# A spatial gate's edge sums on one Trainium2 core: two passes of four-tile groups, or one pass of twelve-tile batches in order of source

## The reference, cut to what matters

```python
h = x @ gcn_w                                   # one score per node
deg = segment_sum(ones, dst) ; dis = rsqrt(deg) # with one more self loop
msg = h[src] * (dis[src] * dis[dst])[:, None]
spa = sigmoid(segment_sum(msg, dst) + gcn_b)
return x * spa + x + x * gate                   # gate: a small MLP on the mean row of x
```

## Time and profile before

| | us |
|---|---|
| median of 3 runs | 8108.09 (8104.7 to 8108.87) |
| the profiled execution's own time | 8111.77 |
| its span (first to last instruction) | 8110.0 |
| mean granted PE clock over the span | 0.731 |

### The profile page before, as it was taken

One profiled execution on the slowest core, in us unless ns is written; L12 is line 12 of the kernel. 1 busy time (PEld: TensorE's weight loads), 2 busy tenths in 40 slices (PEclk: granted clock), 3 DMA queues, 4 the chain that ended last, 5 costly groups with the idle time before them and its releaser, 6 DMA issues. The chain is left out here.

```text
span 8110.0 us, 144759 instructions
## 1 busy us (share of the span) xinstructions
PE 5676.6 (70%) x26332; PEld 3710.7 (46%) x26333; DVE 5077.9 (63%) x16894; ACT 1922.6 (24%) x2930; POOL 4449.1 (55%) x5024
## 2 busy tenths in 40 slices
PE   5566667799999866629999997944555555555550
PEld 4333334477777646516555554522333333333330
DVE  8877777477777579866777775556333333333335
ACT  4100000288888323202333332310000000000000
POOL 0477777377777300002777771001777777777770
PEclk7577777899999865559999999977555555555555
DMA  2244444433333200013333333001111113111122
GB/s 86 59 123 122 123 125 130 117 108 103 103 103 102 50 4 0 0 36 98 104 104 104 104 103 65 0 23 52 52 52 52 52 52 50 52 52 52 52 50 64
DMA packets 306083, 583.62 MB, mean 72 GB/s; under 512 B 88467, under 2 KB 175708, under 8 KB 305562
## 3 DMA queue, kind: packets, MB, share of 16 engines
q0 software_dynamic: 185408, 469.86, 21.3%
q1 hardware_dynamic: 120538, 112.45, 4.5%
HBM read 544.78 MB, written 43.61 MB: 73 GB/s over the span
## 5 line engine op out<-in xcount | busy, mean ns | idle before, releaser
L1591 DVE TENSOR_TENSOR acc<-bank,acc 128x256 f32 (+1 forms) x3552 | 1273.4, 358 | 1725.6 <-PE bank L732 1356.4
L732 PE MATMUL bank<-ring,oh 128*128 128x128 f32 x3552 | 1335.8, 485 | 937.9 <-issue 647.1
L732 PEld LDWEIGHTS bank<-ring,oh 128*128 128x128 f32 x3552 | 885.0, 312 | 1388.8 <-issue 1006.4
L497 POOL CAST stage_i<-s_idx 128x8 int32 (+1 forms) x224 | 46.3, 206 | 1773.3 <-DMA q_table<-hq 1044.9
L512 POOL DMA_INDIRECT ring<-h_table,stage_i x888 | 858.4, 967 | 255.7 <-PE bank L805 149.0
L512 POOL DMA_INDIRECT ring<-fwd_table,stage_i x888 | 847.2, 954 | 261.4 <-issue 230.2
L512 POOL DMA_INDIRECT ring<-bwd_table,stage_i x888 | 847.9, 955 | 258.5 <-issue 232.5
L512 POOL DMA_INDIRECT ring<-q_table,stage_i x888 | 845.2, 952 | 262.5 <-issue 140.7
L1143 ACT ACTIVATE ring<-big 128x889 f16<-128x889 f16 x840 | 874.0, 1041 | 214.1 <-PE bank L816 182.1
L816 PE MATMUL bank<-ring,big 128*128 128x445 f16 (+1 forms) x3360 | 773.7, 352 | 0.0
L1602 DVE TENSOR_SCALAR oh<-iota,d_loc,d_norm 128x128 f32<-128x128 f32 x1776 | 651.8, 370 | 70.1 <-DVE big L1675 20.3
(11 more groups left out here) (394 smaller groups left out, 8402.7 us busy)
## 6 DMA issues: line engine op xcount, KB each, us to landing
big<-places_in_block SPq DMA_DIRECT2D x111, 256.0 KB
ring<-h_table,stage_i POOLq DMA_INDIRECT x888
ring<-q_table,stage_i POOLq DMA_INDIRECT x888
ring<-fwd_table,stage_i POOLq DMA_INDIRECT x888
ring<-bwd_table,stage_i POOLq DMA_INDIRECT x888
big<-x_and_degree,stage_i POOLq DMA_INDIRECT x536
h_table<-hq SPq DMA_DIRECT2D x50, 128.0 KB, 1.7
x_table<-big SPq DMA_DIRECT2D x1, 6400.0 KB, 20.3
```

Source lines behind the costliest of these rows:

```text
L732: pe.matmul(bank[u % 4][:, 0:width], oh[:, u % 4, :], gbuf[:, u % RING, 0:width], start=True, stop=True).then_inc(S["mm"], 1)
L1591: dve.tensor_tensor(to, bank[u % 4][:, 0:width], to, ALU.add).then_inc(S["accd"], 1)
```

## The change

The two passes, `node_values` and `segment_sums` with `combine`, become one pass, `node_sums`, over the list in order of source, in 74 batches of 12 tiles. For each batch: SP loads the 1536 source places to all 128 partitions as a row (`load_slots`, 384 KB, two buffers); DVE compares it with the partition's number (`slot_oh`, one operation of 1536 columns); PE fetches the values with 12 matmuls of three columns at the tile's block (`slot_values`); ACT copies them in pairs (`copy_values`); DVE compares the destination's block (600 columns, `high_eq`) and place (1536 columns, `low_oh`) with `iota`, and multiplies the block one-hot by the three parts of the values in one operation of 12 x 3 x 50 = 1800 columns (`place_values`); PE adds 12 products of 150 columns to `bank[7]` (`slot_sums`). At the end three operations add the three parts.

`read_codes` moves from DVE to POOL in 32-bit float operations, behind POOL's last gather of the second pass: 15 linked operations until `s_ready` is 1, and 7 more until it is 2 (destination's place and block, in pairs). Before the mean's sums PE now clears `bank[7]` and transposes `s_loc` (7 transposes), and ACT copies the result (`slot_w`), ahead of its first square root; SP stores it to `places_in_block`. The scores of a pair are made after the normalisation of the next one (`node_scores(i - 1)` behind `normal_rows(i)`), with waits on semaphores of an earlier turn. `gate_bc` and `gate_done` move behind `spa_in`, and with them SP's load of the next layer's weights.

The core of the diff (the lines between are left out):

```diff
-        code_i = [spare(2 * SLOTS + TC * k, TC)[:, 0:T].bitcast(I32) for k in range(3)]
+        code_f = [spare(2 * SLOTS + TC * k, T) for k in range(3)]
...
+        EDGES = BATCH * P
+        slot_rows, slot_oh = (acc_flat[:, a:a + EDGES].bitcast(BF16).rearrange("p (k n) -> p k n", k=2) for a in (0, EDGES))
...
@@ SP @@
+            sp.wait_ge(S["slot_w_ready"], 2)
+            sp.dma_start(loc_dram.rearrange("(g p n) -> p g n", p=P, n=P), slot_w.rearrange("p (g n) -> p g n", n=P)).then_inc(S["locs_out"], 16)
...
+            def load_slots(i, k, first):
+                if not first:
+                    sp.wait_ge(S["slot_sel"], i * 2 + k - 1)
+                sp.dma_start(slot_rows[:, k, :], loc_dram[ds(i * (2 * EDGES) + k * EDGES, EDGES)].partition_broadcast(P)).then_inc(rows_in[k], 16)
...
             sp.wait_ge(S["gate_done"], 1)
@@ POOL @@
+            pool.wait_ge(S["sort_out"], 4)
+            for k in range(2):
+                link(pool.tensor_tensor(diffs[k], raised[k][:, 1:T + 1], raised[k][:, 0:T], ALU.subtract))
...
+            def by_128(low, high, whole):
+                link(pool.tensor_scalar(high, whole, 1.0 / P, -63.5 / P, ALU.mult, ALU.add))
+                link(pool.tensor_scalar(high, high, ROUND, None, ALU.add))
+                link(pool.tensor_scalar(high, high, ROUND, None, ALU.subtract))
+                link(pool.tensor_scalar(low, high, -float(P), None, ALU.mult))
+                link(pool.tensor_tensor(low, whole, low, ALU.add))
...
+            pool.sem_inc(S["s_ready"], 1)
+            by_128(code_lo, code_hi, s_idx[:, 0:T])
+            for to, code in ((dst_lo, code_lo), (dst_hi, code_hi)):
+                link(pool.tensor_copy(to, code.unsqueeze(2).to_broadcast([P, T, 2])))
+            pool.sem_inc(S["s_ready"], 1)
@@ PE @@
-            def segment_sums(k):
-            def combine(k, turns):
-            def node_values(k):
...
+            def slot_values(i, k):
+                b = i * 2 + k
+                pe.load(slot_regs, blk_s[0:1, ds(i * (2 * BATCH) + k * BATCH, BATCH)])
+                pe.wait_ge(S["slot_sel"], b + 1)
+                pe.wait_ge(S["slot_cp"], b + 1)
+                for u in range(BATCH):
+                    block_no = pe.snap(slot_regs[u], min_val=0, max_val=NB - 1)
+                    mm = pe.matmul(bank[2 + k][:, u * 4:u * 4 + 3], slot_oh[:, k, u * P:(u + 1) * P],
+                                   table3[:, :, ds(block_no, 1)].rearrange("p s a -> p (s a)"), start=True, stop=True)
+                mm.then_inc(S["slot_val"], 1)
+
+            def slot_sums(i, k):
+                pe.wait_ge(S["slot_prod"], i * 2 + k + 1 + 2)
+                for u in range(BATCH):
+                    mm = pe.matmul(bank[7][:, 0:3 * NP], low_oh[k][:, u, :], high_val[k][:, u, :], start=False, stop=False, skip_group_check=True)
+                mm.then_inc(S["slot_acc"], 1)
+
+            def node_sums():
...
+                with pe.Fori(1, BATCHES // 2) as i:
+                    slot_values(i, 0)
+                    slot_sums(i - 1, 1)
+                    slot_values(i, 1)
+                    slot_sums(i, 0)
...
+            pe.wait_ge(S["s_ready"], 1)
+            for g in range(TG):
+                mm = pe.transpose(bank[g // 4][:, g % 4 * P:(g % 4 + 1) * P], s_loc[:, g * P:(g + 1) * P], ident[:, :])
+            mm.then_inc(S["pe_chain"], 1)
+            pe.wait_ge(S["slot_w_ready"], 2)
@@ ACT @@
+            def copy_values(i, k):
+                b = i * 2 + k
+                act.wait_ge(S["slot_val"], b + 1 + 2)
+                act.wait_ge(S["slot_prod"], b + 1)
...
+            act.wait_ge(S["pe_chain"], 1)
+            for h in range(2):
+                n = (4 if h == 0 else TG - 4) * P
+                act.activation(slot_w[:, h * 4 * P:h * 4 * P + n], bank[h][:, 0:n], ACT.Copy).then_inc(S["slot_w_ready"], 1)
             square_root(sm["rstd"][:, 0:NBE])
@@ DVE @@
+            def select_slots(i, k):
+                b = i * 2 + k
+                dve.wait_ge(rows_in[k], i * 16 + LOADED[k] + 16)
+                dve.wait_ge(S["slot_val"], b + 1)
+                dve.tensor_scalar(slot_oh[:, k, :], slot_rows[:, k, :], node_no[:, :], None, ALU.is_equal).then_inc(S["slot_sel"], 1)
+                t = ds(i * (2 * BATCH) + k * BATCH, BATCH)
+                dve.wait_ge(S["slot_acc"], b + 1)
+                dve.tensor_tensor(by_pairs(high_eq[k], NP), iota_pairs(NP), over(dst_hi[:, t, :], NP), ALU.is_equal).then_inc(S["slot_eq"], 1)
+                dve.tensor_tensor(by_pairs(low_oh[k], P), iota_pairs(P), over(dst_lo[:, t, :], P), ALU.is_equal)
+
+            def place_values(i, k):
+                b = i * 2 + k
+                dve.wait_ge(S["slot_cp"], b + 1 + 2)
+                dve.wait_ge(S["slot_eq"], b + 1)
+                o = dve.tensor_tensor(high_val[k].rearrange("p u (s n r) -> p u s n r", s=3, r=2),
+                                      by_pairs(high_eq[k], NP).unsqueeze(2).to_broadcast([P, BATCH, 3, NP // 2, 2]),
+                                      val_pairs[k].unsqueeze(3).to_broadcast([P, BATCH, 3, NP // 2, 2]), ALU.mult)
+                o.then_inc(S["slot_prod"], 1)
...
+                with dve.Fori(1, BATCHES // 2) as i:
+                    select_slots(i, 0)
+                    place_values(i - 1, 1)
+                    select_slots(i, 1)
+                    place_values(i, 0)
...
-            with dve.Fori(0, PAIRS) as i:
-                chain.enter(i, 2)
-                normalize(x_of(i * 2), i * 2)
-                link(normalize(x_of(i * 2 + 1), i * 2 + 1))
-                dve.sem_inc(S["col_ready"], 2)
...
+            with dve.Fori(2, PAIRS) as i:
+                normal_rows(i)
+                node_scores(i - 1)
...
-            read_codes()
...
+            node_sums(sm["hd"], sm["spa"])
```

More of the change, by code:

```diff
@@ L883, in _ @@
             pe.matmul(bank[4][:, 0:D], ones[0:1, :], staged_x[0:1, 1, :], start=True, stop=True).then_inc(S["pe_chain"], 1)
-            node_values(0)
-            segment_sums(0)
-            combine(0, 0)
+            node_sums()
             pe.wait_ge(S["wb_in"], 32 + 48 + 16)
@@ L1062, in copy_windows @@
                 return fills
[L1064 to L1083, removed]
+            def copy_values(i, k):
+                b = i * 2 + k
+                act.wait_ge(S["slot_val"], b + 1 + 2)
+                act.wait_ge(S["slot_prod"], b + 1)
+                parts = bank[2 + k][:, 0:4 * BATCH].rearrange("p (u w) -> p u w", w=4)[:, :, 0:3]
+                act.activation(val_pairs[k], parts.unsqueeze(3).to_broadcast([P, BATCH, 3, 2]), ACT.Copy).then_inc(S["slot_cp"], 1)
             sqrts = [0]
@@ L1258, in _ @@
             dve.sem_inc(S["l2_acc"], 4)
[L1259 to L1260 removed]
+            for n in ("slot_prod", "d_res", "p_split", "g_ag2", "g_xn", "f_res", "f_out"):
                 dve.sem_inc(S[n], 2)
@@ L1539, in combine @@
-            def combine(k, first, last, dst):
-                w = lambda s: tile_sums[:, 0:T, s:s + 1].rearrange("p t a -> p (t a)")
-                link(dve.tensor_copy(val_b[:, 0:T], w(first)))
-                for s in range(first + 1, last + 1):
-                    link(dve.tensor_tensor(val_b[:, 0:T], val_b[:, 0:T], w(s), ALU.add))
-                link(dve.memset(val_b[:, T:TC], 0.0))
-                dve.sem_inc(S["comb_v"], 1)
-                dve.wait_ge(S["comb_done"], k + 1)
-                link(dve.tensor_copy(dst[:, 0:NB], bank[1][:, 0:NB]))
@@ new lines, in node_sums @@
+            def node_sums(values, to):
+                split3(lambda s: table3[:, s, 0:NB], values[:, 0:NB], sm["t_b"][:, 0:NB])
+                dve.sem_inc(S["values_ready"], 1)
+                dve.wait_ge(S["s_ready"], 2)
+                select_slots(0, 0)
+                select_slots(0, 1)
+                place_values(0, 0)
+                with dve.Fori(1, BATCHES // 2) as i:
[3 more added lines that the diff above has]
+                    place_values(i, 0)
+                place_values(BATCHES // 2 - 1, 1)
+                dve.wait_ge(S["slot_acc"], BATCHES + 2)
+                link(dve.tensor_copy(to[:, 0:NB], bank[7][:, 0:NB]))
+                for s in range(1, 3):
+                    link(dve.tensor_tensor(to[:, 0:NB], bank[7][:, s * NP:s * NP + NB], to[:, 0:NB], ALU.add))
@@ L1851, in _ @@
             dve.sem_inc(S["spa_in"], 1)
+            dve.wait_ge(S["pe_chain"], 5)
+            link(dve.tensor_scalar(gate_bc[:, :], bank[4][:, 0:D], 2.0, None, ALU.add))
+            dve.sem_inc(S["gate_done"], 1)
             dve.wait_ge(S["spa_out"], 1)
```

147 lines of the change are left out of this document (61 added, 86 removed).

## The result

The changed kernel takes 7814.64 us (median of 4, 7811.81 to 7819.45) against 8108.48 for the kernel before on the same chip: ratio 0.9638, 95% interval 0.9621 to 0.9655, 294 us less. The forecast was 7829 in a range of 7780 to 7885. The mechanism of the loop came as described. The saving was 15 us larger than the 279 of the sum, and about half of the excess comes from the scores.

What follows compares the result with a forecast made beforehand. DVE was taken as the bound in node_values, in a row of stages one behind the other. 14 - 0.6 + 265.5 = 278.9 us saved gave a median of 7829 us, range 7780 to 7885.

Steps and rivals of the forecast that it cites:

- scores: Score stretch: later scores remove DVE's waits for its own results, 2.31 to 1.73 us a pair, 14 us saved.
- turned places: Ahead of the scores: new clearing, transposes and copies lie mostly under DVE's work; 0.6 us added, between 0 and 3.
- gate chain and loop: From the mean row to the end of `spa`: end at 3253.1 against 3518.6, 265.5 us saved.
- work behind `spa`: Behind the gate: the earlier load of `wbuf` gains nothing, as PE's third layer comes 125 us behind `spa`.
- Codes on POOL: Between POOL's last gather and ACT's first root: 15 operations at 2 us, 30 in all, covered by 133 us idle.
- Gate chain: Behind the mean row: DVE no longer waits, first `place_values` starts at about 2938.7, after register load, 12 fetches and copy.
- Loop: Batch loop: sums lie bare between placement and comparisons, DVE and PE in turn; period 4.25 us, 73 periods 310.3 us.
- PE as the bound: Rival in the batch loop: two register loads and paced fetches make 4.73 us a batch, 35 us more, 7864; chance 0.2.
- half rate: Rival in the placement: the product of 1800 columns takes 2.05 us, 0.95 more a batch, 7898; chance 0.07.
- The sums were not shorter: Rival in the batch loop, claiming shorter sums: the wait halves, 0.84 us less a batch, 61 us less, 7768; chance 0.08.
- row loads: Rival in the batch loop: 384 KB loads set the pace past 8.5 us; 0.02 for slower, 0.03 for part cost.
- The codes did not come late: Rival on POOL, claiming late codes: 15 operations over 8.9 us each, each us beyond costs 15; chance 0.03.

Runs made afterwards that it cites:

- e6_scores_at_once: Changed kernel with each pair's scores again directly behind its own normalisation: ratio 0.9695 to the kernel before, scores 39.5 us against 33.6 unaltered.
- e7_codes_longer: Changed kernel with the split of a code by 128 done five times on POOL, not once: ratio 0.9703 to the kernel before, 9370.25 us.
- e10_codes_on_dve: Changed kernel with the 22 code operations on DVE behind the dense stage, not on POOL: ratio 0.9704 to the kernel before, 9391.95 us.
- e1_eq_first: Changed kernel with the wait for slot_acc behind the block comparison, not ahead of it: ratio 0.9662 to the kernel before, gate 290.9 us against 320.4.
- e2_low_later: Changed kernel with the place comparison and its wait moved behind the placement of the batch before: ratio 0.9618 to the kernel before, gate 237.7 us.
- e5_three_products: Changed kernel with the placement as three products of 600 columns, not one of 1800: ratio 0.9732 to the kernel before, gate 330.2 us against 320.4.
- e9_low_half_fetches: e2_low_later with 6 of the 12 fetch matmuls per batch: ratio 0.9598 to the kernel before, gate 213.0 us.
- e3_half_fetches: Changed kernel with 6 of the 12 fetch matmuls per batch: ratio 0.9705 to the kernel before, gate 318.9 us against 320.4.
- e11_low_later_again: e2_low_later repeated in the group of another changed-kernel run: ratio 0.9625 to the kernel before, gate 237.6 us.
- e0_after: The changed kernel unaltered, measured again on another chip: 9364.86 us, ratio 0.9696 to the kernel before.

## Why the prediction was right, point by point

Against the profiled execution's own time the sum was 278.9 us and 8111.8 - 7812.24 = 299.6 were measured, 20.7 more. Each term:

| term | forecast | measured | beyond the forecast |
|---|---|---|---|
| scores | 14 | 57.66 - 33.65 = 24.0 | +10.0 |
| turned places | -0.6 | 129.7 to 129.6 from staging to scores: 0 | +0.6 |
| gate chain and loop | 265.5 | 589.42 - 320.80 = 268.6 | +3.1 |
| work ahead of the dense stage | 0 | starts 4.2 earlier | +4.2 |
| work behind `spa` | 0 | 2.7 | +2.7 |

The loop, which is most of the saving, came as told. The five terms do not cancel; all err to the same side. But two of them, 6.9 us together, are not explained, and in the scores the gain leans on a change of PE's clock that the prediction did not have.

**Scores.** The mechanism was right (DVE waited for itself) and the size off. I took 1.73 us a pair and it was 1.34. Two readings failed. First, DVE's bare work: 1.51 us was busy time with ends that overlap the next start, and the 0.13 for a loop turn came from a loop of one instruction a turn; the pitches are 0.66 + 0.34 + 0.34, with no turn to be seen. Second, PE's 1.53 us a pair and its 1.87 at the most were taken as constants. They were measured at a granted clock of 0.74 on average; with the pairs closer together PE was granted 0.91 over the stretch and needed 1.20. The gain leans on that rise. In the first 5.7 us of the after trace PE was at 0.50 and, once it had work waiting, a weight load with its matmul came every 0.43 us:

```profile
2867.30:2873.00 5.70, 4.79 (x12) 1.39 (x13) 5.67 (x25) 0.00 (x0) 0.00 (x0) 0.50 0.36 141
2873.00:2879.00 6.00, 5.79 (x25) 1.56 (x23) 6.00 (x29) 0.00 (x0) 0.00 (x0) 0.98 0.00 0
...
2870.29 0.13 PEld L902 LDWEIGHTS bank<-big,ones 128*1 128x1 f32 x1 [0.30 <-issue]
2870.72 0.13 PEld L902 LDWEIGHTS bank<-big,ones 128*1 128x1 f32 x1 [0.30 <-issue]
```

Four of them make 1.72 us a pair, more than DVE's 1.34, so PE fell behind there and caught up once it was granted 1.00. Had it stayed at 0.50, the 100 matmuls would have taken 43 us, 9 more than the stretch, and the mean row waits for them (my estimate from these rows; no run shows it). The whole gain was put down to "the later scores", though most belongs to the dropped link: e6_scores_at_once.

**Codes on POOL.** The 15 operations took 29.1 us (2727.7 to 2756.8) for a forecast of 30, and all 22 were over by 2771.2. That the two agree so well is in part luck: two of the 15 are memsets of 0.1 us, and the other 13 took 2.2 us each for the 2 assumed, from 0.9 to 3.2. The cover was there, as e7_codes_longer and e10_codes_on_dve show, and it is worth 17 us of DVE's time. The estimate from the Trainium skill ("GPSIMD Engine Reference", 3.1 Elementwise), 1.95 us for a two-input operation, agrees: 1.7 to 2.3 in this trace.

**Gate chain.** The first placement came 7.5 us behind the mean row's start, for 9.5 forecast. PE's chain took 5.7 us of them where it had taken 6.9, and the fetches followed it at once: their register load lay under the chain. That is 2.0 of the 3.1 us.

**Loop.** The period was 4.26 us for 4.25. From the end of the placement to the block comparison it was 1.91 for 1.78 + 0.11, of which the selection covers the start and 1.38 are waited; the 0.11 stood in no row. It is shown that the sums lay bare, by e1_eq_first and e2_low_later, and that the placement is on the path, by e5_three_products. The 1.1 us that are left of the 3.1 lie at the ends of the loop: the first period was 5.12 us, the last placement followed the one before it after 1.0, and both batches' sums came together behind it, 3.18 us long. The sum had 73 equal periods.

Two steps were wrong without consequence. One is PE's share: it needed about 3.1 of the 4.26 us, not 4.0. The fetches took 1.54 for 1.57. The register load was sized after one of 8 registers, 0.59; that of 12 came as one load, not two, and took 0.85 (line 722, in ns: least, median, most):

```profile
L722 PEldq TENSOR_LOAD <-blk_s x74: 846/848/859, 2905.4 to 3213.1; - x74
```

But it lay almost whole beside running matmuls, where the sum had it in line with them. The other is DVE's bare work, given as "2.9": the four values named add up to 3.08 with the selection at its bound of 0.72, and e9_low_half_fetches measured 2.78, with the selection at 0.53.

**Rivals.** PE as the bound is refuted by e3_half_fetches. The product did not run at half rate: it took 1.09 us. The sums were not shorter: 1.68 us, at 0.50 throughout. The rule of the Trainium skill ("TensorE: Matmul & The Clock Gate", Part 1), a matmul's time in proportion to the clock, cannot be tested there, as this loop never left that level. The column sums fit it by their starts, one every 0.43 us at 0.50 and every 0.21 at 1.00; their recorded durations, 631 and 377 ns, shrank less. No wait for row loads is in the trace, also not at 3.11 us a batch. The codes did not come late.

**What stays open.** The 4.2 us ahead of the dense stage are there before any changed line runs (the first staging behind the first pass starts at 1504.7 for 1509.6); no run tells run-to-run difference from the layout of the code. The same holds for the 2.7 us behind `spa`.

The experiments point to a faster kernel: e2_low_later, at 0.9618 and 0.9625 of the kernel before, by another order of DVE's operations and no new buffer.

## What to carry to other kernels

Where no engine is busy for over three quarters of a loop, look for the operation whose buffer is freed last and ask what DVE could do ahead of its wait: here moving one comparison behind the placement, and the wait with it, was worth 83 us of the gate, with two buffers as before. Wait at the operation that overwrites the buffer, not at the head of its group. Count the bare work of an engine by pitches, not by busy time. Ask at which clock PE's price was measured, and whether the change will alter that clock.

## What the runs showed of the hardware

- **The same score loop took 1.34 us a pair in ten of the runs and 1.57 in e10_codes_on_dve,** with about 0.2 us between the second score and the next normalisation (3444.51 to 3444.70) and no releaser, at a granted clock of 1.00. The loop's own instructions are the same; what stands ahead of them in DVE's program differs. The price of a DVE loop turn is thus zero or 0.2 for one and the same loop; what decides it is open.
- **POOL's price goes by the form of the operation.** On 888 columns of fp32 in the after trace a multiply with an add took 0.93 to 1.24 us, a single add, subtract or multiply 2.4 to 2.8, a minimum with a multiply 3.19.
- **Single DVE operations grow long beside POOL's.** In the after trace a one-hot of 0.34 us took 1.91 and a product of 0.68 took 1.95 while POOL began its chain. Staging a pair, 0.43 us alone, took up to 1.46 there and up to 2.21 in the eleven other traces with POOL's codes; in the two with POOL idle, that of before and e10_codes_on_dve, the longest was 0.43. The dense stage took it in its slack.
- **PE busy and at the lower level.** In the gate of e11_low_later_again PE was busy for 229.38 of 237.70 us at a granted clock of 0.51, while the column sums just ahead of it, busy for 29.82 of 33.70, had 0.95. Twelve matmuls of 150 columns took 1.68 us at either level.
- **A load of registers by PE's sequencer** took 0.59 us for 8 and 0.85 for 12 (L722), one load each.

```profile
2727.58 1.91 DVE L1612 TENSOR_SCALAR oh<-iota,d_loc,d_norm 128x128 f32<-128x128 f32 x1
2729.41 0.41 DVE L1601 TENSOR_TENSOR acc<-bank,acc 128x256 f32 x1
2729.74 1.95 DVE L1703 TENSOR_TENSOR big<-big,hq 128x512 f32<-128x512 f32 x1
```

- **The same program took 19% longer in all three groups of experiments, and not evenly.** There the gate took its 354 us as before, but all behind `spa` took 5587 to 5644 us in the twelve runs for 4589 in the first profile. In the groups by line the additions of the scatter passes (L1601, 358 ns each in both) stood idle for 2207 us in e0_after against 1710, with 881 against 59 put down to issue. So much of the time goes between instructions. Whether the chip or something else about the first call made it faster is open.
